# A four-pass pipeline over eight images: the experts' tiles spread over 139 steps of shared banks

## The chip, the cores and the metric

The kernel runs on one core of one Trainium2 chip. The metric is the device time of one execution in microseconds (us). The engines are TensorE (PE; its weight loads are a row of their own, PEld), VectorE (DVE), ScalarE (ACT), GpSimd (POOL) and the queue of SyncE (SP), which here only issues DMAs.

## What is computed

Eight images of 48 x 48 tokens (2304 each) with 128 channels go through two layers:

```
x = x + conv_layer(group_norm(x))
    # project to 256 channels, 3x3 depthwise conv, data-dependent decay dt and B, C of 16 states,
    # h = exp(dt*A)*h + dB*x over the 2304 tokens (a scan), y = sum_n h*C + Dskip*x, layer norm, gate, project back
t = t + attention(layer_norm(t))        # linear attention: 8 heads of 16, softmax over q's channels and k's tokens
t = t + experts(layer_norm(t))          # 8 experts, the two best of each token, silu(x W1) * (x W3 + b3), then W2
```

All arithmetic that concerns us is fp32; weights, shapes and results are the same in both kernels.

## The kernel before, in words

**Steps and passes.** The scan of an image is cut into 6 chunks of 384 tokens and 32 row blocks of 8 channels x 16 states, so 192 steps (`SC`) of one 128 x 384 scan each. A pass is 192 steps in which image i is scanned. The program is written out step by step for each engine (`run` in each engine's function): in step k an engine issues what its list says for that step, in that order, and never goes past a wait. Nothing is scheduled at run time; the engines drift apart only as far as their semaphores let them.

**What runs in a pass.** `Around(q, p, j, i, nx)` names five images. Image i is scanned; nx, the next, is turned, group-normed and begins its convolution in the last third; j, the one before i, goes through attention, gating and the sort of its rows by expert (steps 23 to about 190); p and q, two and three before i, go through the experts. An image's own time t runs through the passes: attention's t is k; the experts' t is k + 192 while it is p and k + 384 while it is q. There are a short opening pass (steps 96 to 191), eight full ones (0 to 7; 3 and 4 are the two turns of a hardware loop, run twice so as to give passes 3 to 6), and an `ended` pass without a scan that finishes images 5, 6 and 7. Pass 1 has attention but no experts, pass 2 experts from step 126 on, passes 3 to 7 all of it (pass 7 has no next image).

**The step's core.** PE copies the input rows of step k + 2 into one of three PSUM banks (line 824), first thing in its step k and after scan k - 1 has freed the bank; DVE multiplies it (line 1458) and scans (line 1471); ACT makes the decay three steps ahead (line 1097); POOL multiplies the state by C (line 638); PE folds four of those (line 887). Beside it PE runs 18 taps of convolution per half chunk pair (line 810) and the small projections of the chunk (lines 841 to 873), all in the bank `ps_conv` or `ps_main`.

**The experts.** The sorted rows make 43 tiles (`NU`) of 128 rows, each with one expert. The list `TILE` has 45 places (`NU + LAG`, the last two only to finish): place u at t. There PE at t fills `ps_h` with 3 matmuls and a transpose of a later tile's rows (`tile_up`, lines 977, 966), at t + 1 `ps_g` with 3 matmuls and with 3 more of tile u - 2 (`tile_down`, lines 989, 996). ACT reads `ps_h` at t + 1 (1273, 1276) and `ps_g` at t + 2 (1285, 1291) and issues the weights of tile u + 5 (two DMAs of 384 and 193.5 KB). DVE's silu (1681) at t + 2 reads `ps_h` last and frees it. POOL multiplies both (`hidden`, 745) at t + 3. The places stand at t = 318 to 410, so steps 126 to 191 of pass p (32 of the 45) and 0 to 26 of the next (13); 40 of the 44 distances are 2 steps, four are 3.

**Around them.** POOL scatters the 36 row groups of image j (two per 128 tokens, line 733) at steps 132 to 190; it gathers the results at t = 384 + 34 to 112 (36 gathers, line 756, each pair of groups followed by two sums, 763 and 767). `route` (DVE, steps 114 to 119) finds the two best experts from one bank of logits; the sort (steps 122 to 130) counts them. x of the next image is loaded from step 112 (`load_x`), turned at steps 125 to 135 in `ps_conv` (line 794), normalised at step 145 (`group_norm`), and its first conv taps stand three to a step at steps 147 to 149 and 153 to 155 (`LATE_TAPS`).

**Who may use a bank.** `ps_h` and `ps_g` serve the attention's 49 uses (steps 32 to 121) and the experts' (steps 126 to 26 of the next pass), never both in one stretch. Each use has a number, and waits until the use before it in that bank was read. The numbers are per image, so images that skip uses are corrected by `pass_over`.

Of the kernel before, what the change touches and what calls it, by code (L numbers as in the profile page):

```python
# [130 lines left out]

class Around:
# [23 lines left out]
def build(nc, a):  # L156

    with ExitStack() as ctx:
# [114 lines left out]

        banks = [ps_main, ps_h, ps_g, ps_conv, ps_main, ps_x[0], ps_x[1]]
# [5 lines left out]
        placed += [(f"xT{g}", CB) for g in range(NC)] + [("gm", CB), ("gv", CB)]  # L280
        placed += [(f"conv{hf}{c}", CB) for c in range(NC) for hf in range(HV)]
        attn_uses = list(SEQ) + [f"ek{g}" for g in range(NC)] + ["ctx", "ctx2"] + list(SEQ2)
        attn_uses += [f"uT{g}" for g in range(NC)] + ["logit", "rank"]
        placed += [(name, (HB, GB)[n % 2]) for n, name in enumerate(attn_uses)]
        expert_uses = [("T0", HB), ("T1", HB)] + [(f"h{u}", HB) for u in range(NU)] + [(f"g{u}", GB) for u in range(NU + LAG)]
        placed += [(f"last {name}", (XA, XB2)[n % 2]) for n, name in enumerate(attn_uses)]
# [6 lines left out]
        skipped = [sum(b == x for _, x in expert_uses) for b in range(7)]  # L293
        later = list(aux_per)
        aux_per = [n + m for n, m in zip(aux_per, skipped)]
        for name, b in expert_uses:
            aux_of[name] = (b, aux_per[b] + later[b])
            later[b] += 1
# [3 lines left out]
        attended = tuple(aux_per[b] - skipped[b] for b in range(7))  # L302
# [4 lines left out]
        def use(i, name):  # L307

            if is_last(i) and name in attn_uses:
                return *aux_of[f"last {name}"], 0  # L310
            return *aux_of[name], i
# [312 lines left out]
        def _(pool):  # L624
# [51 lines left out]
            def attention(m, t, scatter):  # L676
# [44 lines left out]
                if t in scatter:  # L721
                    k = scatter.index(t)
# [4 lines left out]
                    if k == NT:  # L727
                        due(pool, s_scatter, m, NT)
                        pool.sem_inc(s_sp.sem, 1)
                        pool.tensor_copy(u_weight, gw[:, 3, :]).then_inc(s_weight.sem, 1)  # L730
                        due(pool, s_weight, m, 1)
                        pool.sem_inc(s_sp.sem, 1)
# [36 lines left out]
            def run(w, first, last):  # L769
                for k in range(first, last):  # L770
# [8 lines left out]
                    attention(w.j, k, T_SCATTER_LAST if w.ended else T_SCATTER)  # L779
# [4 lines left out]
        def _(pe):  # L784
# [3 lines left out]

            def turn(i, g):
                name = f"xT{g}"  # L790
                pe.wait_ge(*free(i, name))
# [99 lines left out]
            def attend(m, name):  # L891

                o = aux(name, m)
                pe.wait_ge(*free(m, name))
# [105 lines left out]
            def attention(m, t):  # L1000
                if m is None:
                    return
# [751 lines left out]
```

## Time and profile before

| | us |
|---|---|
| median of three runs | 4227.19 (4223.45 to 4231.14) |
| the profiled execution, its own time | 4220.52 |
| its span in the profile | 4218.1 |
| PE / DVE / POOL / ACT busy | 3292.7 / 3006.8 / 2917.0 / 2556.1 |
| passes 0, 1, 2 | 355.6, 387.8, 453.4 |
| passes 3, 4, 5, 6 | 488.6, 496.0, 504.4, 495.2 |
| pass 7, and the ended pass | 456.2, 493.9 |

The passes are cut at the first scan (line 1471) of each. A window's row of the profile gives the engines' busy time in it; the passes make stretches of one kernel comparable with one another, because passes 1, 2 and 4 run the same scan with none, some and all of the experts' work beside it.

### The profile page before, as it was taken

The numbers are of one execution on the slowest core, as the hardware profiler recorded it, in microseconds if no ns is written. First come the engines' busy times: TensorE is split into PE (matmuls) and PEld (weight loads), VectorE is DVE, ScalarE is ACT, GpSimd is POOL, SyncE is SP. The second block draws the span as 40 slices with busy tenths as digits, with TensorE's granted clock in tenths as the row PEclk, the third lists the DMA queues.
The fourth block names the chain that finished last, engine by engine and source line by source line (L and its number), as shares of the span: only waits on it lengthen the run. The fifth ranks groups of instructions, "written<-read, shape, count | busy, mean of one in ns | idle before, by whom it ended". The sixth has DMA issues, their size and how long they took to land. (4 is left out here: it accounts for less than half of the span.)

```text
span 4218.1 us, 69032 instructions
## 1 busy us (share of the span) xinstructions
PE 3292.7 (78%) x17432; PEld 1992.9 (47%) x17432; DVE 3006.8 (71%) x5234; ACT 2556.1 (61%) x6173; POOL 2917.0 (69%) x3055
## 2 busy tenths in 40 slices
PE   5687887888788868887788877889778977777473
PEld 2233343344465535653455534555356543557462
DVE  3699998888867977778766877678776788732210
ACT  3465765476567656675566765677556764767352
POOL 1466675867576876779577785768767696857665
PEclk9798997898799978998899987999789998999796
DMA  4865655555677657965678556785668755967584
GB/s 103 194 164 130 150 138 123 142 135 149 174 208 214 156 148 187 240 170 147 161 206 219 146 152 176 210 214 141 163 170 229 195 144 149 250 186 226 152 244 118
DMA packets 420321, 730.04 MB, mean 173 GB/s; under 512 B 56201, under 2 KB 313810, under 8 KB 417746
## 3 DMA queue, kind: packets, MB, share of 16 engines
q1 hardware_dynamic: 302418, 484.12, 46.4%
q10 hardware_dynamic: 99072, 203.47, 16.1%
q0 software_dynamic: 18432, 37.93, 3.3%
q8 instruction: 152, 2.49, 0.3%
q14 instruction: 247, 2.02, 0.2%
HBM read 596.93 MB, written 100.07 MB: 165 GB/s over the span
## 5 line engine op out<-in xcount | busy, mean ns | idle before, releaser
L638 POOL TENSOR_TENSOR prod<-state,c_rep 128x384 f32<-128x384 f32 x1536 | 1530.2, 1002 | 899.3 <-DVE state L1471 867.5
L1471 DVE TENSOR_TENSOR_SCAN state<-dt_rep,carry,ps_x 128x384 f32<-128x384 f32 x1280 | 1284.4, 1003 | 6.5 <-issue 5.1
L1458 DVE TENSOR_TENSOR ps_x<-ps_x,db_rep 128x384 f32<-128x384 f32 x1536 | 854.3, 556 | 457.9 <-PE ps_x L824 417.1
L1097 ACT ACTIVATE dt_rep<-dt_rep,vecs 128x384 f32<-128x384 f32 x1536 | 916.7, 612 | 170.1 <-DMA dt_rep<-dt_dram 91.0
L824 PE MATMUL ps_x<-x_stack,copy 96*128 96x384 bf16 x1536 | 546.6, 357 | 350.1 <-DVE state L1471 344.1
L810 PE MATMUL ps_conv<-gx,w_conv 128*128 128x384 f32 x1728 | 703.9, 528 | 9.2 <-DVE parts L1488 6.0
L824 PEld LDWEIGHTS ps_x<-x_stack,copy 96*128 96x128 bf16 x1536 | 155.8, 102 | 850.3 <-DVE state L1471 606.6
L977 PE MATMUL ps_h<-u_t,w_up 128*128 128x128 f32 x2064 | 330.0, 299 | 220.1 <-DVE silu L1681 206.9
L1285 ACT ACTIVATE g_sb<-ps_g,w_down 128x128 f32<-128x128 f32 x1032 | 303.4, 368 | 211.5 <-PE ps_g L996 178.0
L810 PEld LDWEIGHTS ps_conv<-gx,w_conv 128*128 128x128 f32 x1728 | 321.7, 203 | 226.7 <-issue 120.2
L977 PEld LDWEIGHTS ps_h<-u_t,w_up 128*128 128x128 f32 x2064 | 280.1, 203 | 309.7 <-issue 194.5
L745 POOL TENSOR_TENSOR hidden<-g_sb,silu 128x384 f32<-128x384 f32 x344 | 343.6, 999 | 115.0 <-ACT u_out L1291 103.4
L1681 DVE SCALAR_TENSOR_TENSOR silu<-silu,ps_h 128x384 f32<-128x384 f32 x344 | 185.9, 540 | 317.2 <-ACT silu L1276 305.2
L887 PE MATMUL ps_y<-prod,fold 128*32 128x384 f32 x3072 | 361.5, 545 | 34.6 <-POOL prod L638 34.6
L733 POOL DMA_INDIRECT rows_in<-big_u,row_of x288 | 295.3, 1025 | 63.0 <-issue 51.2
L996 PE MATMUL ps_g<-w_down,hidden 128*128 128x128 f32 x2064 | 299.6, 283 | 35.1 <-POOL hidden L745 28.0
L756 POOL DMA_INDIRECT got<-rows_out,row_of x288 | 283.9, 986 | 61.9 <-issue 38.7
L989 PE MATMUL ps_g<-u_t,w_up 128*128 128x128 f32 x2064 | 307.5, 287 | 9.9 <-ACT u_out L1291 7.9
L989 PEld LDWEIGHTS ps_g<-u_t,w_up 128*128 128x128 f32 x2064 | 287.4, 201 | 48.5 <-issue 23.8
L996 PEld LDWEIGHTS ps_g<-w_down,hidden 128*128 128x128 f32 x2064 | 268.3, 198 | 41.5 <-POOL hidden L745 31.5
L1471 DVE TENSOR_TENSOR_SCAN state<-dt_rep,ps_x 128x384 f32<-128x384 f32 x256 | 241.6, 944 | 15.1 <-ACT carry L1106 15.1
L1273 ACT ACTIVATE u_t<-ps_h 128x128 f32<-128x128 f32 x328 | 89.8, 274 | 195.9 <-PE ps_h L966 179.3
(235 smaller groups left out, 4987.2 us busy)
## 6 DMA issues: line engine op xcount, KB each, us to landing
dt_rep<-dt_dram SPq DMA_DIRECT2D x384, 768.0 KB
w_up<-in_w_exp ACTq DMA_DIRECT2D x344, 384.0 KB
w_down<-in_w_exp ACTq DMA_DIRECT2D x344, 193.5 KB
x_stack<-parts SPq DMA_DIRECT2D x576, 48.0 KB
u_in<-rows_in SPq DMA_DIRECT2D x344, 64.5 KB
rows_out<-u_out SPq DMA_DIRECT2D x344, 64.0 KB
dt_dram<-dt SPq DMA_DIRECT2D x192, 96.0 KB
qv<-in_x SPq DMA_DIRECT2D x48, 192.0 KB
```

The costliest lines, as they stand in the source:

```text
L638: pool.tensor_tensor(prod[:, k % HS, :], state[:, k % HS, :], c_rep[:, c % 2, :], ALU.mult).then_inc(s_prod.sem, 1)
L745: pool.tensor_tensor(hidden[:, u % HID, :], g_sb[:, u % 2, :], silu[:, u % 2, :], ALU.mult).then_inc(s_hidden.sem, 1)
L810: ins = pe.matmul(aux(use)[:, 0:T], w_conv[:, tap, P * hf:P * hf + P], gx[:, ROWS * c + dy:ROWS * c + dy + ROWS, dx:dx + W], start=tap == ...
L824: pe.matmul(ps_x[k % XB][:, 0:T], copy[:, b, :], x_stack[:, c % 2, HV * q + hf, :], start=True, stop=True).then_inc(s_xrep.sem, 1)
L887: ins = pe.matmul(ps_y[32 * q:32 * q + 32, 0:T], fold[:, b, :], prod[:, (QD * m + q) % HS, :], start=b == 0, stop=b == 3)
L977: ins = pe.matmul(aux(name)[:, P * k:P * k + P], w_up[:, u % WA, P * k:P * k + P], u_t[:, u % UT, :], start=True, stop=True)
L989: ins = pe.matmul(aux(name)[:, P * k:P * k + P], w_up[:, u % WA, F + P * k:F + P * k + P], u_t[:, u % UT, :], start=True, stop=True)
L996: ins = pe.matmul(aux(name)[:, F:F + P], hidden[:, v % HID, P * k:P * k + P], w_down[:, v % WB, P * k:P * k + P], start=k == 0, stop=k == ...
L1097: act.activation(dt_rep[:, g % XS, q, :], dt_rep[:, g % XS, q, :], ACT.Exp, scale=decay_rate).then_inc(s_decay.sem, 1)
L1285: ins = act.activation(g_sb[:, u % 2, o], aux(name)[:, o], ACT.Identity, bias=w_down[:, u % WB, F + k:F + k + 1])
L1458: dve.tensor_tensor(x_n, x_n, db_rep[:, c % 2, :], ALU.mult).then_inc(s_inflow.sem, 1)
L1471: dve.tensor_tensor_scan(state[:, k % HS, :], dt_rep[:, g % XS, q, :], ps_x[k % XB][:, 0:T], init, ALU.mult, ALU.add).then_inc(s_state.sem, 1)
```

## The change

1. **The places of the tiles.** `TILE` becomes eleven places among the attention's uses, at steps 82, 85, 88, 91, 94, 97, 100, 105, 110, 117 and 124 of pass p, and 34 from step 131 to step 28 of the next pass (23 and 11): of the 44 distances 10 are 2 steps, 29 are 3, five are 5 or 7. `T_LOAD` and `T_W`, from which rows and weights are loaded, move from t = 303 to 260.
2. **The banks.** All uses of `ps_h` and `ps_g` are numbered together, in the order of the steps of a pass (`shared_uses`); PE takes each with `claim`, which in the first passes steps over the numbers of images that are not there; `pass_over` on ACT goes. Four of the next image's six turns go into these banks, at steps 120, 122, 127 and 128; the other two stay in `ps_conv` (126, 128).
3. **Next image.** Loaded from step 107; group norm at steps 132 to 140 (was 138 to 145); first taps at most two to a step, from steps 141 to 145 and 150 to 155.
4. **Logits and sort.** The logits come in two halves (steps 113 to 115 and 120 to 122), which ACT copies out of PSUM and DVE searches in SBUF at steps 118, 119, 124 to 127; the sort stands at 130 to 138. The turns of u stand at 103, 103, 108, 108, 113, 115 (were 102 to 107).
5. **Scatter and gather.** The scatter's first 18 stand at steps 140 to 174, the second 18 at 180 to 191 and, as image p, at 0 to 22 of the next pass. The gathers leave out steps 53 to 65 and, but for seconds, 82 to 96.
6. **The ended pass.** The scatter is 18 + 18 in a row with no gather between (steps 140 to 176). Image 6's tiles run at 1.5 of its t per step from step 34, then hold; its gathers start at step 179, and image 7's tiles stand from step 184, so all 36 gathers of image 6 lie beside image 7's first two dozen tiles.

```diff
-T_TURN = tuple(NB * TURN - 3 + 2 * g for g in range(NC))
-T_XLOAD = NB * TURN - 16
-LATE_TAPS = ((19, 19, 19, 20, 20, 20, 21, 21, 21), (25, 25, 25, 26, 26, 26, 27, 27, 27))
-LATE_READ = (22, 28)
+EARLY = 4
+T_TURN = (120, 122, 127, 128, 126, 128)
+T_XLOAD = 107
+T_GM, T_GV, T_GN = 4, 7, 12
+LATE_TAPS = ((13, 13, 14, 14, 15, 16, 16, 17, 17), (22, 22, 23, 24, 24, 25, 25, 26, 27))
+LATE_READ = (18, 28)
...
+AMONG = (82, 85, 88, 91, 94, 97, 100, 105, 110, 117, 124)
+T_AMONG, T_LAST = 131, 220
+REST = NU + LAG - len(AMONG)
+TILE = tuple(SC + t for t in AMONG) + tuple(SC + T_AMONG + (T_LAST - T_AMONG) * u // (REST - 1) for u in range(REST))
+T_TILE = TILE[0]
+T_LOAD = T_W = T_TILE - 14
+
+T_GATHER = tuple(2 * SC + t for t in (34, 37, 40, 43, 46, 49, 52, 66, 69, 72, 75, 78, 81, 97, 101, 105, 109, 113))
...
+T_SCATTER = tuple(140 + 2 * k for k in range(NT)) + tuple(180 + 2 * k for k in range(NT))
+T_SCATTER_LAST = tuple(140 + k for k in range(NT)) + tuple(159 + k for k in range(NT))
+T_HOLD, SOONEST = T_GATHER[0] - 1, 282
+ENDED, RESUMED = 34, T_SCATTER_LAST[-1] + 2
...
+def shared_uses(k):
+    uses = [(name, 3) for name in expert_uses(k + 2 * SC)] + [(name, 2) for name in expert_uses(k + SC)]
+    uses += [(name, 1) for name in AT if AT[name] == k]
+    return uses + [(f"xT{g}", -1) for g in range(EARLY) if T_TURN[g] == k]
...
         if self.ended:
-            return (self.q, k + 2 * SC), (self.p, k + SC + SOONER), (self.j, k - SC + SOONEST)
+            own = [min(T_HOLD, T_W + 3 * (n - ENDED) // 2) + max(0, n - RESUMED) for n in (k, k + 1)]
+            return ((self.q, k + 2 * SC), *((self.p, t) for t in range(*own) if k >= ENDED), (self.j, k - SC + SOONEST))
...
+            def claim(m, name):
+                b, k, i = use(m, name)
+                if without.get(b, 0):
+                    pe.wait_ge(aux_free[b].sem, aux_free[b].at(i, k - without[b]))
+                    pe.sem_inc(aux_full[b].sem, without[b])
+                    pe.sem_inc(aux_free[b].sem, without[b])
+                    without[b] = 0
+                pe.wait_ge(*free(m, name))
...
-                    attention(w.j, k, T_SCATTER_LAST if w.ended else T_SCATTER)
+                    attention(w.j, k)
+                    scatter(w.j, k, T_SCATTER_LAST if w.ended else T_SCATTER)
+                    scatter(w.p, k + SC, T_SCATTER)
```

## Rows read from the trace of the kernel before

**Rows 1.** The page: span, busy times, and one of the costliest groups.
```profile
span 4218.1 us, 69032 instructions
...
PE 3292.7 (78%) x17432; PEld 1992.9 (47%) x17432; DVE 3006.8 (71%) x5234; ACT 2556.1 (61%) x6173; POOL 2917.0 (69%) x3055
...
L1458 DVE TENSOR_TENSOR ps_x<-ps_x,db_rep 128x384 f32<-128x384 f32 x1536 | 854.3, 556 | 457.9 <-PE ps_x L824 417.1
```

**Rows 2.** Windows: stretch, us, busy by engine (instructions), clock, DMA; passes 1, 4, ended.
```profile
442.60:830.40 387.80, 312.94 (x1364) 149.16 (x1364) 348.59 (x611) 239.81 (x510) 271.70 (x282) 0.87 0.56 137
...
1772.40:2268.40 496.00, 404.51 (x2186) 249.35 (x2184) 378.75 (x654) 317.10 (x770) 364.40 (x383) 0.90 0.70 181
...
3724.20:4218.10 493.90, 299.03 (x2180) 260.98 (x2179) 86.62 (x230) 236.48 (x720) 310.51 (x348) 0.84 0.61 184
```

**Rows 3.** Windows: steps 80 to 127, 128 to 191, 0 to 23, each in passes 1, 4.
```profile
593.30:703.20 109.90, 81.50 (x338) 37.24 (x338) 97.43 (x222) 63.20 (x144) 67.85 (x80) 0.82 0.53 135
1951.90:2084.10 132.20, 89.09 (x350) 43.71 (x348) 99.11 (x223) 65.25 (x151) 94.10 (x109) 0.78 0.56 147
703.20:830.40 127.20, 99.29 (x371) 42.69 (x370) 111.66 (x175) 65.58 (x136) 104.66 (x102) 0.81 0.57 137
2084.10:2268.40 184.30, 155.70 (x954) 108.43 (x954) 132.64 (x206) 118.78 (x316) 137.08 (x136) 0.94 0.81 216
442.60:481.50 38.90, 36.58 (x150) 16.04 (x150) 37.22 (x61) 24.54 (x48) 27.41 (x27) 0.92 0.65 158
1772.40:1837.10 64.70, 59.56 (x363) 40.42 (x362) 44.36 (x72) 45.71 (x118) 39.82 (x43) 0.97 0.79 205
```

**Rows 4.** Waits in steps 128 to 191 of pass 4: total, times, longest.
```profile
DVE ps_x L1458 <- PE ps_x L824: 29.9, 25, 3.1
PE ps_h L977 <- DVE silu L1681: 27.3, 16, 4.9
...
POOL big_u L730 <- DMA rows_in<-big_u,row_of: 5.6, 1, 5.6
```

**Rows 5.** PE in order of time, one tile's matmuls in that stretch (start, us).
```profile
2131.57 0.83 PE L977 MATMUL ps_h<-u_t,w_up 128*128 128x128 f32 x6
...
2133.18 0.83 PE L996 MATMUL ps_g<-w_down,hidden 128*128 128x128 f32 x6
2133.85 0.49 PE L873 MATMUL ps_main<-dt,w_n 128*128 128x384 f32 x1
```

**Rows 6.** The chain that ended last: a tile's matmuls at the lower clock.
```profile
3606.55 1.28 PE ps_g L989 x6
3607.83 1.28 PE ps_g L996 x6
```

**Rows 7.** Windows: steps 88 to 95 in passes 1 and 4, 144 to 151 in pass 1.
```profile
607.50:624.50 17.00, 7.92 (x32) 1.99 (x31) 15.91 (x36) 13.16 (x31) 17.00 (x19) 0.76 0.37 93
1970.60:1995.80 25.20, 11.58 (x37) 2.83 (x35) 16.43 (x37) 16.68 (x39) 24.50 (x27) 0.64 0.37 81
735.70:755.10 19.40, 16.63 (x67) 8.09 (x65) 15.81 (x25) 6.28 (x14) 16.55 (x15) 0.91 0.45 110
```

**Rows 8.** In order of time, pass 4: ACT's first use of the t1 that SP loads.
```profile
1846.80 1.26 ACT L1233 ACTIVATE big_u<-big_u,nb,r 128x128 f32<-128x128 f32 x3 [0.43 <-DMA big_u<-t_dram]
```

**Rows 9.** POOL in order of time, ended pass: first and last scatters, last tile's product.
```profile
3951.28 1.03 POOL L733 DMA_INDIRECT rows_in<-big_u,row_of  x1 [0.15 <-issue]
...
4013.53 0.98 POOL L733 DMA_INDIRECT rows_in<-big_u,row_of  x1 [0.30 <-issue]
4014.81 0.96 POOL L733 DMA_INDIRECT rows_in<-big_u,row_of  x1 [0.30 <-issue]
...
4148.64 0.99 POOL L745 TENSOR_TENSOR hidden<-g_sb,silu 128x384 f32<-128x384 f32 x1 [1.84 <-ACT u_out L1291]
```

**Rows 10.** POOL in order of time, ended pass: the first tile of image 7; a sum.
```profile
4027.88 0.99 POOL L745 TENSOR_TENSOR hidden<-g_sb,silu 128x384 f32<-128x384 f32 x1
...
4167.49 0.72 POOL L767 TENSOR_TENSOR acc_in<-acc_in,got 128x256 f32<-128x256 f32 x1
```

More of the change, by code:

```diff
@@ L291, in build, with side @@
             aux_per[b] += 1
[L293 to L298, printed above, removed]
+        def side(name):
+            return (HB, GB)[SIDE[name] if name in SIDE else name[0] == "g" or name == "T1"]
+        order = [use for k in range(SC) for use in shared_uses(k)]
+        for b in (HB, GB):
+            aux_per[b] = sum(side(name) == b for name, _ in order)
+        at_place = [0] * 7
+        for name, after in order:
+            b = side(name)
+            aux_of[name] = (b, (after + 1) * aux_per[b] + at_place[b])
+            at_place[b] += 1
+        ended, final_of = Around(B - 3, B - 2, B - 1, None, None), {}
+        at_place = [(B + 1) * n for n in aux_per]
+        for k in range(T_END):
+            for m, t in ended.experts(k):
+                for name in expert_uses(t):
+                    b = side(name)
+                    final_of[(m, name)] = (b, at_place[b])
+                    at_place[b] += 1
         bank_names = ("main", "h", "g", "conv", "end", "last_a", "last_b")
@@ L674, in offsets, with attention @@
                 pool.tensor_tensor(nb[:, :], mv[:, :, 0], r1[:, :], ALU.mult).then_inc(s_coef.sem, 1)
-            def attention(m, t, scatter):
+            def attention(m, t):
                 if m is None:
@@ L1001, in attention @@
                 if m is None:
+                    for name in AT:
+                        if AT[name] == t:
+                            without[side(name)] += 1
                     return
-                if 0 <= t - T_SEQ < len(SEQ):
-                    attend(m, SEQ[t - T_SEQ])
-                if 0 <= t - T_EK < NC:
-                    attend(m, f"ek{t - T_EK}")
+                for name in AT:
+                    if AT[name] == t and name not in ("ctx", "ctx2", "lg0", "lg1", "rank"):
+                        attend(m, name)
                 if 0 <= t - T_CTX < 3:
@@ L1024, in experts @@
                 if m is None:
+                    for name in expert_uses(t):
+                        without[side(name)] += 1
                     return
@@ L1043, in run @@
                         fold_quad(w, (k - FOLD_LAG - QD) // QD)
-                    if w.nx is not None:
-                        if k in T_TURN:
-                            turn(w.nx, T_TURN.index(k))
-                        if c == TURN and n in (10, 13):
-                            group_norm(w.nx, (n - 10) // 3)
+                    for g in range(NC):
+                        if k == T_TURN[g] and w.nx is not None:
+                            turn(w.nx, g)
+                        elif k == T_TURN[g] and g < EARLY and not w.ended:
+                            without[side(f"xT{g}")] += 1
+                    if w.nx is not None and c == TURN and n in (T_GM, T_GV):
+                        group_norm(w.nx, (T_GM, T_GV).index(n))
                     i, cc = w.cell(c + 2)
@@ L1306, in attention @@
                     normalise(m, 0, t - T_NORM, u_tok, u_tok)
-                if 0 <= t - T_SEQ - 1 < len(SEQ):
-                    attend(m, SEQ[t - T_SEQ - 1])
+                for name in AT:
+                    if AT[name] == t - 1 and name not in ("ctx", "ctx2", "lg0", "lg1", "rank"):
+                        attend(m, name)
                 if t == T_KEXP:
@@ L1373, in run @@
                     if w.nx is not None:
-                        if k - 1 in T_TURN:
-                            turn(w.nx, T_TURN.index(k - 1))
+                        for g in range(NC):
+                            if k - 1 == T_TURN[g]:
+                                turn(w.nx, g)
                         if c == TURN:
@@ L1654, in attention @@
                         row_stats(m, acc, g)
[L1655 to L1656 removed]
+                if t in T_ROUTE:
+                    route(m, T_ROUTE.index(t))
                 if t == T_SORT:
@@ L1711, in run @@
                         experts(m, t)
-                    attention(w.j, k, None if w.ended else w.q)
+                    attention(w.j, k, w.q)
             passes(dve, run)
```

176 lines of the change are left out of this document (87 added, 89 removed).

## The prediction

> **What bounds the kernel now.** I read the page first: no engine is full. PE is busy 78% of the span, DVE 71%, POOL 69% [rows 1]. The costliest wait is at the scan: DVE's multiply waits 417.1 us for PE's copy into `ps_x` [rows 1]. That is the kernel's lost time: DVE carries the scan, and PE is late with its input.
>
> Next the windows by pass. Pass 1 (no experts) takes 387.8 us with DVE busy 348.6, 90% of it. Pass 4 (everything) takes 496.0 with DVE busy 378.8, 76% [rows 2]. So the other images' experts add 108.2 us, of which DVE's own work is only 30.2; the rest is DVE idle. The stretches say where [rows 3]: steps 128 to 191 grow by 57.1 us (127.2 to 184.3), steps 0 to 23 by 25.8, steps 80 to 127 by 22.3, and what is left for steps 24 to 79 is 3.0. The first two are where the tiles stand, two steps apart. The third holds no tile: there POOL is busy 94.1 us against 67.9, with the gathers.
>
> Why a tile costs so much is in the waits: in steps 128 to 191 DVE waits 29.9 us for the copy and PE waits 27.3 us for DVE's silu before it may refill `ps_h` [rows 4]. At distance 2 the silu of a tile and the next tile's first matmul stand in the same step: PE stops for DVE, then does its step late, and DVE then stops for PE.
>
> **The change part by part.** Prices are for pass 4 unless said.
>
> (a) Tiles in steps 128 to 191. Now 32 places cost 57.1 us, 1.78 each. Of this DVE busy is 132.64 - 111.66 = 21.0, so 0.66 a tile; idle rises from 15.5 to 51.7, so 1.13 a tile. After the change 23 places stand there, mostly 3 apart, where the silu is one step before the refill. The idle part I take at half, 0.57, so 1.2 a tile: 27.6 us. Gain 29.5. The bounds of that price are 0.66 (idle goes wholly) and 1.78 (it stays). Half is near neither end; I take it since a quarter of the distances is still 2 and since PE's own work stays: a tile starts its matmuls at 2131.57 and is done with them at 2133.85 but for a copy between, 19 instructions at 0.112 us (six from 2133.18 to 2133.85), 2.13 us of PE at full clock [rows 5].
>
> (b) Steps 0 to 28: now 25.8 us, after it 11 places at 1.2, 13.2. Gain 12.6.
>
> (c) The eleven places among the attention, steps 82 to 124: nothing stands there now, so the price is not in the trace. Below: 0.66, DVE's part. Above: PE at the lower clock, 1.28 us per six instructions [rows 6], so 19 x 0.213 = 4.05. Steps 80 to 127 have room, PE busy 89.1 of 132.2 us and DVE 99.1 [rows 3], and distances are 3 to 7, so I take the same 1.2: cost 13.2 us. POOL's eleven products go to places partly vacated by gathers, see (d).
>
> (d) POOL in steps 88 to 95 is busy 24.5 of 25.2 us, against 17.0 us for the same steps without gathers [rows 7]: there POOL is the bound and 8.2 us are lost. The gathers leave these steps, three tile products of 1.0 us come, and two more gathers than before land on steps 34 to 83, where POOL has room. Gain 3; bounds 0 and 8.
>
> (e) Taps and next image. Steps 144 to 151 take 19.4 us in pass 1, where DVE is busy 15.8 and PE 16.6 [rows 7]: 18 taps in nine steps. Spread over steps 141 to 155 I gain 4, bounded by 0 and DVE's idle 3.6 (plus what the same bunch costs in 152 to 155, of the same kind). The four turns that change banks cost the same; their cover is PE's room before step 128.
>
> (f) Logits, route and sort are moved and cut in two; DVE does the same work but for one copy that goes to ACT, and the steps are DVE-bound before and after, so 0, bounds -3 and +5. What queues behind the sort is the scatter, which moves with it, and group norm and sort now stand on DVE in the same steps, 130 to 140.
>
> (g) An added wait. SP's load of t1 at step 25 waits for all scatters of the image before, and the last scatter now stands at step 22 of that pass instead of step 190. ACT's normalise at step 29 already waits 0.43 us for that load [rows 8], so no slack is left: the load comes later by the landing of the last scatter (a wait on such a landing is 5.6 us long [rows 4]), some 4 us as I take it. Behind ACT's wait stands the decay, three steps ahead of the scan. Cost 2, bounds 0 and 5.
>
> A full pass: -29.5 - 12.6 + 13.2 - 3 - 4 + 0 + 2 = -34. Passes 3 to 6: 4 x -34 = -136. Pass 7 has no next image, so no (e), and its tiles stretch is already shorter: -25. Pass 2 has no tail of tiles and no gathers: -29.5 + 13.2 - 4 = -20. Passes 0 and 1: only (e), -4 each.
>
> (h) The ended pass, 493.9 us [rows 2]. Eleven leftover tiles instead of thirteen: -3. The scatter runs from 3951.28 to 4015.8, 64.5 us, with gathers between; after it 36 at the pace 1.28 (4013.53 to 4014.81) [rows 9], 46, plus the wait for the first half's landing, 6: -12.5. Image 7's tiles take 120.8 us for 42 distances, 2.87 each (4027.88 to 4148.64) [rows 9, 10], paced by PE and ACT. All 36 gathers of image 6 now lie beside them: in the first six distances POOL has 1.0 + 2 x 1.2 + 0.73 (half of the two sums of 0.72 per pair [rows 10]) = 4.1 us a tile, +8; in the next four, 12 gathers and six sums, 22 us against 11.5, +11; later none. Then the last gathers, 65 us, lose a little waiting: -3. Sum 0 - 3 - 12.5 + 19 - 3 = about 0; with the gathers' own landings 5 more: +5, bounds -20 and +40.
>
> Sum: -136 - 25 - 20 - 8 + 5 = -184. Against this execution's own 4220.5 us that is 4036.5; the median of the runs shown lies 6.7 above it, so **4043 us**. The likeliest case's own range is 3960 to 4140.
>
> On the clock: where PE has little to do its granted clock is low, 0.64 in steps 88 to 95 with PE busy 11.6 of 25.2 us, while the dense stretches have 0.94 and 0.97 [rows 3, 7]. The Trainium skill ("TensorE: Matmul & The Clock Gate", section on HAM oscillation) says that gaps between bursts of matmuls bring the array back to half clock, which speaks against thinning out a dense stretch. By that rule every tile would run part of its time at half speed and (a) and (b) would give less; by the trace the thin stretches gain PE work too, and this rule's own case is the fourth rival.
>
> **The rivals.**
> 1. *A tile costs the same wherever it stands* (1.8 us at distance 3 too, since PE's 2.13 us of issue are the cost and not the wait). For: PE is the busiest engine. Against: DVE idles 51.7 us in a stretch where PE is busy 155.7 of 184.3. Then only (d), (e), (g) are left: with -5 x 6 - 8 + 5 = -33, 4194 us.
> 2. *All idle goes* (0.66 a tile): another 0.54 x 45 = 24 less in each of six passes, -146: 3897 us. For: DVE fills 90% of pass 1. Against: PE's main-bank bursts stay.
> 3. *The change doesn't do what it says*: the image's tiles, gathers and sort still meet at some one wait in every step, and the time stays at 4227.
> 4. *Slower.* The eleven tiles among the attention run at the lower clock, 4.05 us each, in the order of one queue with attention's uses of the same two banks; PE is late there and the copy behind it too. 2.85 more a tile and 1 us of waiting for the bank: +42 a pass, +252 over six, so 4043 + 252 = 4295 us. It decides from the point where a tile there costs more than 1.2 + 184 / 66 = 4.0 us. For: that clock of 0.64 to 0.8. Against: adding the tiles raises PE's share there.
>
> **How the numbers follow.** Forecast 0.67, rival 1 0.13, rival 2 0.10, rival 3 0.03, rival 4 0.07. What a measurement can tell from no change is 0.2%, 8 us. Faster takes the forecast and rivals 1 and 2: 0.90; same 0.03; slower 0.07. The range is 3940 to 4175: below, it cuts off most of rival 2, above, rival 4 and the upper half of rival 1.
>
> **What would show it.** Passes 3 to 6 at about 462 us each, DVE busy unchanged near 378; in steps 128 to 191 PE's wait for silu and DVE's wait for the copy about halved, 162 us for the stretch instead of 184; steps 0 to 23 at about 53; steps 80 to 127 not above 135; the clock in steps 88 to 95 above 0.64; the image 7 tiles slower at first than 2.87 us apart. I am wrong if steps 80 to 127 grow by over 30 us, if the wait for silu stays at 27 us, or if ACT's normalise waits over 6 us for its load in each pass.

## The result, and the profile after

The changed kernel takes 4011.76 us (median of four runs, 4009.66 to 4013.45) against 4228.67 us in the same comparison: ratio 0.9481, 95% interval 0.9460 to 0.9502. Forecast was 4043 with a range of 3940 to 4175. Its profiled execution has a span of 4011.6 us.

The page of the changed kernel, the lines that answer to [rows 1]:

```profile
span 4011.6 us, 69162 instructions
...
PE 3217.3 (80%) x17432; PEld 1979.4 (49%) x17432; DVE 2970.2 (74%) x5226; ACT 2571.5 (64%) x6203; POOL 2913.6 (73%) x3055
...
L1522 DVE TENSOR_TENSOR ps_x<-ps_x,db_rep 128x384 f32<-128x384 f32 x1536 | 851.1, 554 | 301.3 <-PE ps_x L895 284.5
```

The gain is mostly waiting: DVE is busy 36.6 us less, and its wait for PE's copy into `ps_x` fell by 132.6 us (284.5 for 417.1).

Windows of the changed kernel: pass 1, pass 4, the ended pass; then steps 80 to 127, 128 to 191 and 0 to 23, each in passes 1 and 4; then steps 88 to 95 in pass 4 (columns as in [rows 2], the stretches as in [rows 2, 3, 7]).

```profile
442.00:818.90 376.90, 307.07 (x1363) 147.15 (x1362) 347.07 (x609) 240.75 (x512) 261.63 (x272) 0.88 0.57 139
1706.20:2168.40 462.20, 396.35 (x2184) 248.73 (x2182) 372.04 (x653) 319.76 (x776) 365.94 (x384) 0.92 0.74 194
3511.50:4011.60 500.10, 296.12 (x2127) 259.82 (x2125) 85.89 (x227) 232.58 (x705) 319.15 (x357) 0.84 0.60 179
595.20:694.70 99.50, 74.17 (x342) 35.05 (x340) 90.69 (x210) 64.57 (x148) 67.93 (x80) 0.88 0.58 148
1877.40:2003.40 126.00, 103.10 (x547) 64.44 (x547) 97.22 (x220) 88.04 (x219) 102.75 (x119) 0.87 0.75 202
694.70:818.90 124.20, 96.46 (x368) 40.46 (x366) 116.75 (x186) 65.04 (x135) 94.59 (x92) 0.82 0.57 136
2003.40:2168.40 165.00, 140.14 (x803) 92.70 (x802) 129.16 (x209) 102.37 (x268) 117.61 (x116) 0.92 0.76 201
442.00:481.20 39.20, 36.88 (x150) 16.13 (x150) 37.24 (x61) 24.66 (x48) 27.40 (x27) 0.91 0.66 157
1706.20:1761.00 54.80, 51.71 (x314) 34.12 (x313) 42.46 (x69) 40.86 (x102) 46.31 (x47) 1.00 0.84 221
1903.20:1922.70 19.50, 14.91 (x78) 9.68 (x79) 17.05 (x39) 16.40 (x47) 19.24 (x21) 0.76 0.53 147
```

By pass, in us (each pass cut at its first scan):

| | before | after | difference | forecast |
|---|---|---|---|---|
| opening pass and start | 87.0 | 84.4 | -2.6 | 0 |
| passes 0, 1 | 355.6, 387.8 | 357.6, 376.9 | +2.0, -10.9 | -4 each |
| pass 2 | 453.4 | 433.2 | -20.2 | -20 |
| passes 3 to 6, mean | 496.05 | 458.1 | -37.9 each | -34 each |
| pass 7 | 456.2 | 426.9 | -29.3 | -25 |
| ended pass | 493.9 | 500.1 | +6.2 | +5 |

The sum is -206.5, against -184 forecast. From pass 2 on each line is within 5 us of its forecast; passes 0 and 1 are near it only when added up. The stretches inside a pass fit less well: steps 80 to 127 of pass 1 fell by 10.4 us (109.9 to 99.5), where I forecast nothing. So the question for the experiments was which of the parts had earned the gain, since a sum may be right by errors that cancel.

### The profile page after: what moved, and what is told of

The parts are those of the page before. It is cut to its first block, busy times and chain, and to the rows that moved or that the text cites. A ratio compares the mean times of both kernels' runs of the same rounds, so it can differ in the third digit from the quotient of the medians.

```text
span 4011.6 us, 69162 instructions
## 1 busy us (share of the span) xinstructions
PE 3217.3 (80%) x17432; PEld 1979.4 (49%) x17432; DVE 2970.2 (74%) x5226; ACT 2571.5 (64%) x6203; POOL 2913.6 (73%) x3055
## 3 DMA queue, kind: packets, MB, share of 16 engines
q1 hardware_dynamic: 302418, 484.12, 49.4%
## 4 chain that ended last, share of the span: by engine, by line
PE 32%; issue 18%; DVE 16%; POOL 14%; ACT 11%; DMA 4%; ACTq 2%; SPq 1%; DVEq 0%; POOLq 0%
PE ps_conv L881 7%; DVE state L1535 6%; POOL prod L688 5%; PE ps_main L944 5%; DVE ps_x L1522 4%; PE ps_h L1050 3%; PE ps_g L1062 3%; PE ps_y L958 3%; PE ps_g L1069 3%; POOL got L811 2%; PE ps_x L895 2%; ACT dt_rep L1173 2%; DMA dt_rep<-dt_dram 2%; POOL rows_in L788 2%; ACT big_u L1309 1%
## 5 line engine op out<-in xcount | busy, mean ns | idle before, releaser
L1522 DVE TENSOR_TENSOR ps_x<-ps_x,db_rep 128x384 f32<-128x384 f32 x1536 | 851.1, 554 | 301.3 <-PE ps_x L895 284.5
L895 PE MATMUL ps_x<-x_stack,copy 96*128 96x384 bf16 x1536 | 534.3, 349 | 318.3 <-DVE state L1535 313.9
L881 PE MATMUL ps_conv<-gx,w_conv 128*128 128x384 f32 x1728 | 689.5, 515 | 9.0 <-DVE gx L1510 6.3
L881 PEld LDWEIGHTS ps_conv<-gx,w_conv 128*128 128x128 f32 x1728 | 312.5, 199 | 226.3 <-issue 129.8
L958 PE MATMUL ps_y<-prod,fold 128*32 128x384 f32 x3072 | 351.4, 531 | 8.9 <-POOL prod L688 8.7
L1062 PE MATMUL ps_g<-u_t,w_up 128*128 128x128 f32 x2064 | 313.4, 291 | 26.2 <-ACT u_out L1367 13.3
L1062 PEld LDWEIGHTS ps_g<-u_t,w_up 128*128 128x128 f32 x2064 | 290.3, 204 | 74.4 <-ACT u_out L1367 30.3
L1069 PEld LDWEIGHTS ps_g<-w_down,hidden 128*128 128x128 f32 x2064 | 277.5, 204 | 11.2 <-ACT u_out L1367 7.9
```

Of the source, the lines that this page charges most:

```text
L881: ins = pe.matmul(aux(use)[:, 0:T], w_conv[:, tap, P * hf:P * hf + P], gx[:, ROWS * c + dy:ROWS * c + dy + ROWS, dx:dx + W], start=tap == ...
L895: pe.matmul(ps_x[k % XB][:, 0:T], copy[:, b, :], x_stack[:, c % 2, HV * q + hf, :], start=True, stop=True).then_inc(s_xrep.sem, 1)
L958: ins = pe.matmul(ps_y[32 * q:32 * q + 32, 0:T], fold[:, b, :], prod[:, (QD * m + q) % HS, :], start=b == 0, stop=b == 3)
L1062: ins = pe.matmul(aux(name)[:, P * k:P * k + P], w_up[:, u % WA, F + P * k:F + P * k + P], u_t[:, u % UT, :], start=True, stop=True)
L1069: ins = pe.matmul(aux(name)[:, F:F + P], hidden[:, v % HID, P * k:P * k + P], w_down[:, v % WB, P * k:P * k + P], start=k == 0, stop=k == ...
L1522: dve.tensor_tensor(x_n, x_n, db_rep[:, c % 2, :], ALU.mult).then_inc(s_inflow.sem, 1)
```

## The experiments

All are edits of the changed kernel but where said otherwise, each timed in three rounds beside the kernel before. The passes come from one profiled execution of each: the mean of passes 3 to 6, where the changed kernel has 458.1, and pass 1, where it has 376.9. Pass 1 holds no tiles and no gathers, and in the four runs that move only these (e1, e3, e5, e6) it took 375.8 to 377.0 us, which says how far such a figure can be trusted. The runs were timed in three groups on three chips (e1 to e4, e5 to e8, e9 to e11), so whole times are compared by their ratios. In e1, e2 and e8 the ended pass is longer too (521.1, 521.2 and 527.2 us for 500.1), because its tiles stand elsewhere too; so the parts are priced by passes 3 to 6. Most expectations set two theories against each other; they are called the first and the second.

| run | median us | ratio to the kernel before (95%) | passes 3 to 6 | pass 1 |
|---|---|---|---|---|
| e1_old_places | 4124.2 | 0.9758 (0.9716 to 0.9800) | 474.8 | 376.8 |
| e2_old_route | 4184.3 | 0.9897 (0.9846 to 0.9948) | 481.7 | 389.8 |
| e3_dense_rest | 4071.1 | 0.9628 (0.9592 to 0.9664) | 467.8 | 377.0 |
| e4_one_scatter | 4047.6 | 0.9569 (0.9533 to 0.9605) | 464.5 | 386.3 |
| e5_old_gather | 4040.1 | 0.9571 (0.9543 to 0.9600) | 465.1 | 376.0 |
| e6_gather_late | 3970.7 | 0.9407 (0.9379 to 0.9434) | 451.8 | 375.8 |
| e7_old_taps | 3988.1 | 0.9451 (0.9421 to 0.9481) | 453.1 | 379.1 |
| e8_old_turns | 4130.7 | 0.9785 (0.9753 to 0.9816) | 477.7 | 379.0 |
| e9_late_old_taps | 3951.4 | 0.9373 (0.9337 to 0.9408) | 447.8 | 379.1 |
| e10_later_still | 3962.7 | 0.9391 (0.9359 to 0.9423) | 448.6 | 379.4 |
| e11_conv_bank | 3987.9 | 0.9452 (0.9419 to 0.9485) | 452.5 | 379.2 |

**The tiles at their old places.**

```diff
-TILE = tuple(SC + t for t in AMONG) + tuple(SC + T_AMONG + (T_LAST - T_AMONG) * u // (REST - 1) for u in range(REST))
+TILE = tuple(318 + 92 * u // (NU + LAG - 1) for u in range(NU + LAG))
```

> The changed kernel with the 45 tile places of the kernel before (t = 318 to 410, distance 2, none among the attention's uses); all else as changed. Read by passes 3 to 6, since the ended pass also shifts. If distance is what sets a tile's price (the prediction's 1.78 at distance 2 and 1.2 at distance 3), these passes rise from 458 to about 485, and steps 128 to 191 back to 184. If a tile costs 1.8 at either distance in a full stretch and only the eleven among the attention are cheap (26.5 us over pass 1 in steps 80 to 127 with tiles, 22.3 without), steps 128 to 191 rise by 16, steps 0 to 31 by about 5, steps 80 to 127 fall by about 6: passes of about 473.

Passes 3 to 6 rose by 16.7 us to 474.8. The second theory's number was 473, the first one's, which is the prediction's, 485. Windows of pass 4 of this run: the pass, steps 80 to 127, 128 to 191, 0 to 31:

```profile
1724.20:2198.80 474.60, 397.18 (x2186) 246.18 (x2185) 372.42 (x653) 315.41 (x771) 364.60 (x383) 0.91 0.71 189
1900.50:2013.00 112.50, 78.97 (x346) 38.40 (x344) 91.47 (x209) 65.14 (x151) 92.13 (x107) 0.83 0.65 173
2013.00:2198.80 185.80, 158.63 (x957) 110.26 (x958) 134.03 (x218) 117.29 (x316) 125.21 (x124) 0.93 0.76 209
1724.20:1801.60 77.40, 68.02 (x406) 44.27 (x405) 56.88 (x92) 58.53 (x150) 61.56 (x70) 0.95 0.81 219
```

Steps 80 to 127 are 13.5 us shorter than in the changed kernel (112.5 for 126.0): the eleven tiles there cost 1.2 us each. Steps 128 to 191 are 20.8 longer. Over passes 3 to 6, the 45 tiles outside the attention cost 86.8 us over pass 1, 1.93 each; the changed kernel's 34 cost 56.6, 1.66 each. Both theories were half right: the eleven moved tiles are cheap, and those left also got cheaper, but by 0.27 and not by 0.6. In pass 4 alone, from which (a) was priced, steps 128 to 191 of the changed kernel show no cheaper tile at all: 40.8 us over pass 1 for 23 tiles, 1.77 each, against 1.78 before. PE is busy 43.7 us more there than in pass 1, 1.90 a tile.

**Distance alone.**

```diff
-T_AMONG, T_LAST = 131, 220
+T_AMONG, T_LAST = 131, 198
```

> The changed kernel with the 34 later tile places on steps 131 to 198 (distance 2) instead of 131 to 220; the eleven among the attention stay. If distance 2 costs 0.57 us more a tile because PE waits for the silu, passes 3 to 6 rise by 19 us to 477, and PE's wait for the silu in steps 128 to 191 goes from 15 to over 27 us. If a tile's price is the same, the passes stay within 4 us of 458, with steps 128 to 191 longer by about 18 and steps 0 to 31 shorter by as much.

Passes 3 to 6 rose by 9.7, halfway between. With the 34 tiles at distance 2 the price is 1.92 (65.3 us over pass 1), the same as with 45. So distance is worth some 0.26 us a tile at 34 tiles. The waits in steps 128 to 191 of pass 4, of the changed kernel and of this one (total, times, longest):

```profile
DVE ps_x L1522 <- PE ps_x L895: 20.0, 20, 5.7
PE ps_h L1050 <- DVE silu L1744: 15.1, 8, 5.1
```

```profile
DVE ps_x L1522 <- PE ps_x L895: 33.3, 28, 4.2
PE ps_h L1050 <- DVE silu L1744: 21.3, 14, 3.6
```

The first window holds 23 tiles and the second 30, so the totals have to be read per tile: the wait for the silu is 0.66 us a tile at the wider distance, 0.71 here and 0.85 before (27.3 for 32 tiles, [rows 4]); DVE's wait for the copy is 0.87, 1.11 and 0.93. That is a small change for a wait that was to be halved. PE in order of time in the changed kernel shows whose wait it is (start, us; in brackets the idle time before), at places 133, 141, 144, 149 and 174 of pass 4:

```profile
2018.41 0.58 PE L1050 MATMUL ps_h<-u_t,w_up 128*128 128x128 f32 x1 [3.02 <-DVE silu L1744]
...
2043.71 0.58 PE L1050 MATMUL ps_h<-u_t,w_up 128*128 128x128 f32 x1 [5.07 <-DVE silu L1744]
...
2056.22 0.38 PE L1050 MATMUL ps_h<-u_t,w_up 128*128 128x128 f32 x2
...
2071.50 0.71 PE L1050 MATMUL ps_h<-u_t,w_up 128*128 128x128 f32 x4 [2.55 <-DVE silu L1744]
...
2126.01 0.37 PE L1050 MATMUL ps_h<-u_t,w_up 128*128 128x128 f32 x1 [1.68 <-DVE silu L1744]
```

The first, second and fourth stand 2 steps after the tile before. The seven tiles of this stretch at distance 2 hold 12.6 of the 15.1 us; of the fifteen at distance 3 only two wait more than 0.3 us (1.68 and 0.56). So at distance 3 the wait is gone, as forecast. But the few tiles left at distance 2 wait 1.8 us each, more than one did before, and the two longest waits are at steps 133 and 141, among the sort and the group norm and just behind them. And a tile still costs 1.7 us: most of the idle time that I had put down to this wait is not its work. What is left is in proportion to the tiles, as PE's own work of 1.90 us in each would be; no run here tried that alone.

**Route, and the turns of u.** On top of the first run:

```diff
-T_UT, T_LOGIT = (103, 103, 108, 108, 113, 115), (113, 120)
-T_ROUTE = (118, 119, 124, 125, 126, 127)
-T_RANK, T_SORT = 129, 130
+T_UT, T_LOGIT = (102, 103, 104, 105, 106, 107), (108, 111)
+T_ROUTE = (114, 115, 116, 117, 118, 119)
+T_RANK, T_SORT = 121, 122
```

> As the run before it, and the turns of u back at steps 102 to 107, the two halves of the logits at 108 and 111, route at 114 to 119, rank 121, sort 122. Compared with the run before it. Pass 1 of the changed kernel was 10.4 us shorter in steps 80 to 127 than before, which the prediction had at 0. If the spacing of u's turns, logits and route is the cause, pass 1 rises by about 10 us in steps 80 to 127 and so do passes 3 to 6. If it is something else (the copy of the logits by ACT, the next image's earlier load), pass 1 stays within 2 us.

Pass 1 rose by 13.0 us and passes 3 to 6 by 6.9, where the first theory had about 10 for both. Only the turns, same base:

```diff
-T_UT, T_LOGIT = (103, 103, 108, 108, 113, 115), (113, 120)
+T_UT, T_LOGIT = (102, 103, 104, 105, 106, 107), (113, 120)
```

> The changed kernel with the tile places of before (as the first run of these) and only the turns of u back at steps 102 to 107; logits, route and sort as changed. The second run moved all of these back and pass 1 rose by 13.0 us, passes 3 to 6 by 6.9. If the turns, which wait for ACT's normalise in PE's queue, are half of it (steps 104 to 107 of pass 1 took 13.3 instead of 7.8 us), pass 1 rises by 5 to 6 us over the first run. If all of it is route and sort, it stays within 1.

Pass 1 rose by 2.2 and passes 3 to 6 by 2.9: less than the 5 to 6 I expected, so most of it is in logits, route and sort. The ratios of this run and of the first overlap; it is steps 88 to 127 that show it, 2.1 us longer in pass 1 and 3.1 in passes 3 to 6. Steps 88 to 127 of pass 1, of the first run, of this one, and of the run with all of it moved back:

```profile
605.40:690.30 84.90, 59.98 (x281) 28.35 (x279) 76.40 (x181) 56.66 (x129) 56.55 (x63) 0.86 0.54 139
```

```profile
602.60:689.60 87.00, 62.86 (x281) 28.88 (x279) 76.41 (x181) 56.56 (x129) 56.58 (x63) 0.85 0.54 135
```

```profile
602.70:705.90 103.20, 74.15 (x284) 36.16 (x283) 82.43 (x194) 57.01 (x129) 56.65 (x63) 0.74 0.45 113
```

DVE has 6.0 us more to do in the last, the part of the sort that now falls in, but the stretch is 18.3 us longer, and the rest of the pass gives back only 5.3: idle time grew from 8.5 to 20.8. Which of logits, route and sort it is was not taken apart further.

**The scatter.**

```diff
-T_SCATTER = tuple(140 + 2 * k for k in range(NT)) + tuple(180 + 2 * k for k in range(NT))
+T_SCATTER = tuple(140 + 51 * k // (NSC - 1) for k in range(NSC))
```

> The changed kernel with all 36 scatters at steps 140 to 191 of the attention's own pass, as before the change in kind. By the prediction's parts the two placements cost the same but for the wait of SP's load at step 25, so passes 3 to 6 lose 2 us or nothing. If POOL is near its bound where the second half stood before (pass 1 was 5.6 us shorter in steps 176 to 191 after the change), steps 128 to 191 rise by 5 to 8 us, steps 0 to 31 fall by some 5, and the pass as a whole moves by less than 4.

A miss: I expected under 4 us for the pass, and passes 3 to 6 rose by 6.4, pass 1 by 9.4, pass 7 by 12.9; only pass 2 fell, by 4.9. Steps 176 to 191 of pass 1, of this run and of the changed kernel:

```profile
788.70:822.30 33.60, 24.18 (x94) 11.21 (x93) 26.44 (x43) 13.36 (x29) 30.32 (x31) 0.80 0.56 137
```

```profile
792.90:818.90 26.00, 19.39 (x89) 8.12 (x88) 25.95 (x43) 13.27 (x29) 24.57 (x26) 0.91 0.59 144
```

In this run POOL is busy 30.3 of 33.6 us there, and DVE idles 7.2 (0.05 in the changed kernel). POOL's share alone would not tell, since it is as high in the changed kernel; the waits do. In this run PE waits for POOL's product of the state, and DVE waits 4.2 us for PE's copy behind it:

```profile
PE ps_y L958 <- POOL prod L688: 4.7, 3, 2.1
```

So what these steps gain is that five scatters leave them (31 instructions on POOL, then 26). This run is not the old placement, though: that had the 36 scatters at steps 132 to 190, and this one, behind the later sort, has them closer together, at 140 to 191. Of the 7.6 us that these steps lose in it, 5.6 stand in the kernel before too (31.6 us for 26.0); the other 2.0 may be the closer spacing. In steps 0 to 31 of passes 3 to 6, where the second half goes in the changed kernel, little is gained back by taking it out (71.0 for 71.8): PE is busy 51.7 of the 54.8 us of steps 0 to 23 there and POOL 46.3, so I take it that PE sets the pace.

**The gathers.**

```diff
-T_GATHER = tuple(2 * SC + t for t in (34, 37, 40, 43, 46, 49, 52, 66, 69, 72, 75, 78, 81, 97, 101, 105, 109, 113))
+T_GATHER = tuple(2 * SC + 34 + 23 * x // 5 for x in range(NT))
```

> The changed kernel with the gathers at the places of the kernel before (34 to 112, 4.6 apart), through steps 84 to 96. By the prediction's part (d) keeping the gathers out of steps 84 to 96 gains 3 us a pass (0 to 8), so passes 3 to 6 go from 458 to about 461. If POOL's places matter more, because three tile products now stand there too, steps 80 to 127 rise by 8 or more and the pass to 466. If only the sum of POOL's work in steps 80 to 127 counts, nothing moves.

They cost 7.0 us a pass, the second theory's size, but not all in its place: over passes 3 to 6 steps 80 to 127 rose by 4.3 us and steps 24 to 79 by 2.7. Then the other way, two pairs of them moved out of the steps that had become the slowest:

```diff
-T_GATHER = tuple(2 * SC + t for t in (34, 37, 40, 43, 46, 49, 52, 66, 69, 72, 75, 78, 81, 97, 101, 105, 109, 113))
+T_GATHER = tuple(2 * SC + t for t in (34, 37, 40, 43, 46, 49, 52, 66, 69, 72, 75, 97, 101, 105, 109, 113, 120, 124))
```

> The changed kernel with the two pairs of gathers at steps 78 to 83 moved to 120 to 126, where POOL is busy 1.2 of 2.5 us a step. In the changed kernel steps 80 to 87 take 25.8 us (14.3 in pass 1), with ACT waiting 7.1 us for POOL's spread of the row statistics of step 82, and DVE's silu behind it. If POOL's queue there is the cause, steps 80 to 87 fall by about 5 us, each of passes 3 to 7 by 5, and the time by 25 us to about 3987. If the first tile's own handshake is the cause (the same steps took 18.7 before the change and no tile stood there), steps 80 to 87 stay at 25 and the time within 5 us of 4012.

Steps 80 to 87 of pass 4, window and then waits, of the changed kernel and after it of this one:

```profile
1877.40:1903.20 25.80, 19.87 (x97) 11.70 (x98) 15.65 (x32) 13.36 (x31) 24.14 (x33) 0.93 0.85 235
```

```profile
ACT r L1299 <- POOL mv L718: 7.1, 1, 7.1
DVE silu L1744 <- ACT silu L1352: 7.1, 1, 7.1
```

```profile
1866.50:1886.30 19.80, 17.84 (x97) 11.13 (x98) 15.53 (x32) 13.43 (x31) 18.86 (x27) 1.00 0.96 257
```

```profile
ACT r L1299 <- POOL mv L718: 3.6, 1, 3.6
DVE silu L1744 <- ACT silu L1352: 1.9, 1, 1.9
```

Six instructions less on POOL, 6.0 us less for the steps; the wait of ACT, and of DVE behind it, halved or better. Passes 3 to 6 fell by 6.4 to 451.8 and pass 7 by 7.1. The median fell by 41 us, where 25 was expected: five passes give 33 of it, and pass 0 and the start, which the edit doesn't touch, differ by another 8.5 between the two executions, so I count those as spread. By the ratios (0.9407 for 0.9481) the gain is 31 us.

But the gathers alone don't make these steps slow. In the run with the old tile places they stand at steps 78 to 83 as well, with no tile beside them. Steps 80 to 87 of its pass 4, and ACT's wait in them:

```profile
1900.50:1919.90 19.40, 15.86 (x61) 8.60 (x60) 14.77 (x29) 4.24 (x11) 17.55 (x23) 0.82 0.71 201
```

```profile
ACT r L1299 <- POOL mv L718: 11.6, 1, 11.6
```

There ACT waits longer for the same statistic, and the steps take 19.4 us; before the change it waited 11.3 us, and they took 18.7. What the change added is a tile at step 85, whose silu on ACT stands in the queue behind two such waits; DVE waits for it, and the scan behind DVE. ACT in the changed kernel, in order of time:

```profile
1892.97 0.31 ACT L1299 ACTIVATE r<-mv,vecs 128x18 f32<-128x18 f32 x1 [7.05 <-POOL mv L718]
...
1898.46 1.26 ACT L1309 ACTIVATE big_k<-big_k,nb,r 128x128 f32<-128x128 f32 x3 [2.35 <-POOL nb L724]
...
1901.72 0.48 ACT L1352 ACTIVATE silu<-ps_h 128x384 f32<-128x384 f32 x1
```

So it takes both, a late POOL and a tile behind it, and half of the price of the eleven stands in these steps: the two tiles at 82 and 85 cost 6.7 us together (steps 80 to 87 over passes 3 to 6, against the run with the old places), the nine in steps 88 to 124 cost 7.1, 0.8 each. With the gathers moved, all eleven cost 7.5 us, 0.7 each, near DVE's own part of 0.66 (both tile placements with late gathers were not compared).

**Group norm and the next image's first taps.**

```diff
-T_GM, T_GV, T_GN = 4, 7, 12
-LATE_TAPS = ((13, 13, 14, 14, 15, 16, 16, 17, 17), (22, 22, 23, 24, 24, 25, 25, 26, 27))
-LATE_READ = (18, 28)
+T_GM, T_GV, T_GN = 10, 13, 17
+LATE_TAPS = ((19, 19, 19, 20, 20, 20, 21, 21, 21), (25, 25, 25, 26, 26, 26, 27, 27, 27))
+LATE_READ = (22, 28)
```

> The changed kernel with the group norm at steps 138 to 145 and the next image's first taps three to a step at 147 to 149 and 153 to 155, as before. By the prediction's part (e) spreading them gains 4 us a pass: passes 1 and 3 to 6 rise by 4 us, in steps 144 to 159, the time by some 24 us. If DVE's load with sort and group norm in the same steps 130 to 140 is the dearer thing, undoing it gains, steps 128 to 143 fall by 3 or more and the pass moves by less than 2.

The prediction's part has 4 us a pass more, and it is 5.1 less. The second theory named the right steps, but expected the pass to move by less than 2. The ratios of this run and of the changed kernel overlap (0.9421 to 0.9481, 0.9460 to 0.9502), so the reading rests on the steps. Steps 128 to 143 of pass 4, the changed kernel and this one:

```profile
2003.40:2054.80 51.40, 38.66 (x184) 24.75 (x184) 40.22 (x69) 28.67 (x70) 26.87 (x25) 0.78 0.59 155
```

```profile
1988.20:2033.10 44.90, 33.60 (x175) 21.59 (x175) 37.57 (x67) 27.32 (x66) 24.25 (x25) 0.84 0.64 167
```

The stretch is 6.5 us shorter, steps 144 to 175 only 1.7 longer (76.7 for 75.0). In pass 1, with no tiles, undoing costs 2.2. Steps 128 to 143 and 144 to 159 of pass 1, of the changed kernel and then of this one:

```profile
694.70:736.10 41.40, 27.71 (x90) 11.17 (x89) 37.98 (x64) 19.21 (x39) 21.36 (x20) 0.67 0.44 106
736.10:766.60 30.50, 25.05 (x103) 11.52 (x102) 27.35 (x45) 14.63 (x32) 24.31 (x24) 0.89 0.53 126
```

```profile
687.90:724.40 36.50, 24.74 (x83) 9.63 (x82) 35.35 (x62) 18.78 (x39) 17.86 (x17) 0.67 0.49 117
724.40:761.50 37.10, 26.63 (x110) 12.37 (x109) 30.87 (x46) 15.01 (x33) 27.59 (x26) 0.93 0.44 105
```

So the crowd at steps 128 to 143 costs about as much with tiles as without (6.0 us over passes 3 to 6, 4.9 in pass 1). What differs is the worth of spreading the taps: 6.6 us in pass 1 and 0.8 over passes 3 to 6. The edit moves both, so which of the two acts is read off the steps; neither was moved alone.

**The best parts together.** The last two edits in one kernel (e9), and then with two more pairs of gathers later (e10), at (..., 97, 101, 113, 116, 119, 122, 125):

> The two improving edits together: a pair of gathers moved from steps 78 to 83 to 120 to 126, and group norm and first taps of the next image back at the places of the kernel before. Alone they gave 3970.7 and 3988.1 us against 4011.8, so 41 and 24 less. If their gains lie in different steps (80 to 87 and 128 to 143) and add up, the time is about 3947 us and passes 3 to 6 are about 446. If the gathers now at 120 to 126 delay what stands at 128 to 143, part of the second gain is lost: 3960.

> As the run before it, and the gathers of steps 105 and 109 moved too, so that five stand at 113 to 125. Steps 88 to 127 of pass 4 took 100 us against 85 in pass 1, with seven tiles and six gathers. If POOL's queue is what is late there, they fall by 3 us and the time by 15 to about 3932. If PE's tiles are the price, nothing moves; if sums and gathers crowd steps 113 to 131, it rises by up to 10.

The gains add up, nearly: 3951.4 us where 3947 was expected, passes 3 to 6 at 447.8 for 446, ratio 0.9373 against 0.9481 for the changed kernel, the intervals well apart. Moving more gathers gained nothing (0.9391, within e9's interval; passes 3 to 6 at 448.6 for 447.8): steps 88 to 127 rest on something else, which stays open.

**The bank of the turns.** Against e7:

```diff
-EARLY = 4
-T_TURN = (120, 122, 127, 128, 126, 128)
+EARLY = 0
+T_TURN = (125, 127, 129, 131, 133, 135)
```

> The changed kernel with group norm and first taps at their places of before and all six turns of the next image back in the convolution's bank, at steps 125 to 135. Against the run that moved only group norm and taps (3988.1 us, passes 3 to 6 at 453). If the bank and place of the turns are worth nothing, as the prediction had it, it is within 8 us of 3988. If the turns at 127 and 128 cost, because their banks are held by the tile of step 124 and the rank until DVE has read, passes 3 to 6 get shorter by 2 to 4 us; if turning late costs DVE's statistics next to the sort, longer by as much.

Nothing: 3987.9 for 3988.1, and 452.5 for 453.1 us in passes 3 to 6. The turns in the shared banks are worth nothing by themselves; they only make the earlier group norm possible, and that is no gain in a full pass.

## Why the prediction was right

Its sign, its size and the passes from 2 on are right, and the measured time is 31 us below the forecast. Of the terms of a full pass only (c) has the right number, and the errors of the others cancel. That their sum, 34 us, came so near the measured 37.9 is luck: undone one at a time, tiles, gathers and taps give 16.7, 7.0 and -5.1 where the terms had 28.9, 3 and 4, and 13.3 come from two parts that had 0.

- **(a), (b) a tile at distance 3, 1.2 us: too low.** It is 1.66 with all that steps 0 to 31 hold, 1.92 at distance 2, so the idle part went by 0.27 and not by 0.57. The mechanism is there, but small: at distance 3 PE no longer waits for the silu, while over all the 23 tiles of the stretch that wait fell only from 0.85 to 0.66 us a tile. The step that failed is the size, half of the idle time; most of that time came from something else. By [rows 3] and the windows after, steps 128 to 191 gained 19.3 us where (a) alone had 29.5; steps 0 to 31 gained 5.8 where (b) had 12.6.
- **(c) 1.2 us for each of the eleven: right as a sum**, 13.5 / 11 = 1.2, but made of nine at 0.8 and two that cost 6.7 together, by a meeting with the gathers that I had not seen.
- **(d) 3 us for the gathers: too low.** Undoing costs 7.0, near the upper bound of 8. The bound of a POOL-bound stretch was in the rows (8.2 us); I took the middle. And two pairs of gathers at steps 78 to 83 stand on POOL just ahead of the statistics that ACT waits for, now with a tile's silu behind ACT's wait: steps 80 to 87 rose from 18.7 to 25.8 us. I had called that place "room", by POOL's share of the stretch and not by what is queued behind.
- **(e) a gain of 4 us for taps and group norm: wrong sign in a full pass**, where it is a loss of 5.1; in pass 1 it is a gain of 2.2. I saw in (f) that group norm and sort meet in steps 130 to 140, and gave it no price. The 4 was also above the bound of 3.6 that I worked out beside it.
- **(f) 0 for logits, route and sort: too low**, 6.9 us of passes 3 to 6 and 13.0 in pass 1, of which the turns of u 2.9 and 2.2. I judged the steps DVE-bound by their busy share, and missed the idle time in the steps around them. Pass 1 fell by 10.9 and not by 4 for this and the scatter. There the parts don't add up, though: undone one by one they give 13.0, 9.4 and 2.2, which is 24.6.
- **The scatter, priced at nothing, is worth 6.4 us a pass** against all 36 at steps 140 to 191 (against the old places, 132 to 190, it was not measured): the second half left steps where POOL was late.
- **(g) the added wait, 2 us: hardly seen.** ACT's first normalise of pass 4 waits for nothing where it waited 0.43 us [rows 8] (idle before it would stand in brackets), in pass 3 it waits 0.70 where it waited for nothing, and without the second half of the scatter steps 0 to 31 are only 0.8 shorter:

```profile
1774.08 1.25 ACT L1309 ACTIVATE big_u<-big_u,nb,r 128x128 f32<-128x128 f32 x3
```

- **(h) the ended pass: right, nearly term by term**, but for the first. Until the first scatter it takes 230.6 us, 3.5 more and not 3 less. The scatters take 49.4 us (forecast 52), the tiles 144.8 (forecast 120.8 + 19, and 5 for the gathers' landings), and between the two lie 8.4 us for 12.1, which I had not counted. POOL's order of time shows it, to be held against [rows 9, 10]:

```profile
3742.11 1.03 POOL L788 DMA_INDIRECT rows_in<-big_u,row_of  x1 [2.17 <-issue]
...
3790.58 0.96 POOL L788 DMA_INDIRECT rows_in<-big_u,row_of  x1 [0.30 <-issue]
...
3799.93 1.00 POOL L800 TENSOR_TENSOR hidden<-g_sb,silu 128x384 f32<-128x384 f32 x1
...
3944.68 0.99 POOL L800 TENSOR_TENSOR hidden<-g_sb,silu 128x384 f32<-128x384 f32 x1 [1.83 <-ACT u_out L1367]
```

The parts undone one by one give, for passes 3 to 6: places 16.7, route and turns 6.9, scatter 6.4, gathers 7.0, taps and group norm -5.1; 31.9 of the 37.9. The other 6 stay open: interactions, or the copy of the logits by ACT and the earlier load of x, which were not tried alone. One number points at the parts that no run undid: DVE is busy 371.9 us in a pass for 378.5 before (mean of passes 3 to 6), and in the eleven runs it is 369.5 to 372.9 whatever was moved back. That this shortens the pass by as much is not shown.

The first and the fourth rival are settled by e1. A tile doesn't cost the same everywhere (1.2 among the attention, 1.7 to 1.9 elsewhere), though outside the attention the first rival was nearer than the forecast. And the eleven didn't run cold: steps 88 to 95 rose from a granted clock of 0.64 [rows 7] to 0.76, and pass 4 as a whole from 0.90 to 0.92. The second rival, all idle time gone, falls with the price of 1.66 for its 0.66. Of the stretches that lost tiles, steps 0 to 23 rose from 0.97 to 1.00 and steps 128 to 191 fell from 0.94 to 0.92. The rule that spoke against thinning out ("TensorE: Matmul & The Clock Gate" of the Trainium skill, section on HAM oscillation) did not bite here: the small fall is not the thinning's, as the last section shows.

## What to carry to other kernels

In this pipeline, written out by steps, the place of a tile was worth more than its distance (0.4 to 1 us against 0.27). To find such places, compare a pass with and without the work, stretch by stretch, to get a price per unit in each place. Give each moved item a price on every queue it enters, and ask what it stands behind: here ACT's wait of 11 us for a statistic had not stopped DVE until a tile's silu came to stand behind it; then it cost 6 us. When a forecast fits, undo its parts one at a time all the same; here one of five parts cost 5 us a pass and hid behind the others, and taking it back, with one more move, brought the ratio from 0.9481 to 0.9373, some 46 us (the medians differ by 60).

## What had not been expected of the hardware

Where the dense stretch was thinned, the granted clock of steps 0 to 23 of pass 4 went from 0.97 to 1.00: fewer matmuls, but in a shorter time, with PE busy 51.7 of 54.8 us, for 59.6 of 64.7 before. In steps 128 to 143 it fell from 0.89 to 0.78, with PE busy 38.7 of 51.4 us. That looks like the price of thinning, and is not. These steps in the kernel before, in the run with the old, dense tile places (e1), and in the run with the sort moved back as well (e2):

```profile
2084.10:2129.40 45.30, 36.11 (x223) 25.44 (x224) 35.47 (x58) 32.41 (x81) 31.25 (x31) 0.89 0.83 220
```

```profile
2013.00:2072.70 59.70, 45.96 (x236) 31.77 (x237) 41.51 (x71) 33.61 (x86) 29.00 (x27) 0.78 0.61 166
```

```profile
2058.90:2110.10 51.20, 38.68 (x229) 27.57 (x230) 35.84 (x58) 33.43 (x85) 28.18 (x27) 0.87 0.74 199
```

With the tiles dense again the clock stays at 0.78, and with the sort elsewhere it is back at 0.87; with the group norm later instead it is 0.84 (PE busy 33.6 of 44.9 us). So the lower clock goes with DVE's crowd of sort and group norm beside the matmuls, and not with the number of tiles.
